# A graph network kernel: the second layer's first two pairs of tiles are taken into the first stage

## The reference

```python
def gat_conv(x, src, dst, W, a_src, a_dst, bias):      # H = 4 heads, C = 256
    h = (x @ W).reshape(n, H, C)
    al_s = jnp.einsum('nhc,hc->nh', h, a_src)
    al_d = jnp.einsum('nhc,hc->nh', h, a_dst)
    e = jax.nn.leaky_relu(al_s[src] + al_d[dst], NEG_SLOPE)
    ...                                                # softmax over the edges of each dst: alpha
    out = jax.ops.segment_sum(h[src] * alpha[:, :, None], dst, num_segments=n)
    return out.reshape(n, H * C) + bias
...
h = jax.nn.relu(gat_conv(x, src, dst, W1, a_src1, a_dst1, b1))   # src, dst with a self loop per node
h = jax.nn.relu(gat_conv(h, src, dst, W2, a_src2, a_dst2, b2))
return h @ Wfc + bfc
```

## Time and profile before

| | before |
|---|---|
| median of 3 runs | 2270.3 us (2266.53 to 2275.2) |
| the profiled execution | 2270.06 us |
| its span in the profile | 2268.0 us |
| PE busy | 2203.5 us (97%) |
| DVE busy | 1487.4 us (66%) |
| ACT busy | 1017.8 us (45%) |
| POOL busy | 944.5 us (42%) |
| mean granted clock of PE | 0.989 |

### The profile page before, as it was taken

One profiled execution on the slowest core, in us unless ns is written; L12 is line 12 of the kernel. 1 busy time (PEld: TensorE's weight loads), 2 busy tenths in 40 slices (PEclk: granted clock), 3 DMA queues, 4 the chain that ended last, 5 costly groups with the idle time before them and its releaser, 6 DMA issues.

```text
span 2268.0 us, 36374 instructions
## 1 busy us (share of the span) xinstructions
PE 2203.5 (97%) x12269; PEld 1889.0 (83%) x12269; DVE 1487.4 (66%) x4613; ACT 1017.8 (45%) x2024; POOL 944.5 (42%) x931
## 2 busy tenths in 40 slices
PE   7999999979999999999999999999999999999996
PEld 6878788858899888888999999988888777888785
DVE  7777778755667856666435665277776766677675
ACT  4982112222356632222224665334344665666454
POOL 2017637745222234366542222023545553652542
PEclk9999999989999999999999999999999999999998
DMA  6334575443476748787225666356667776776532
GB/s 211 140 136 138 133 203 193 163 138 105 137 246 216 272 158 275 258 284 244 86 88 187 214 233 237 126 195 210 229 206 255 239 241 218 242 249 222 170 123 65
DMA packets 192479, 435.82 MB, mean 192 GB/s; under 512 B 45735, under 2 KB 74606, under 8 KB 191758
## 3 DMA queue, kind: packets, MB, share of 16 engines
q1 hardware_dynamic: 127018, 249.08, 32.0%
q0 software_dynamic: 65296, 184.67, 26.2%
HBM read 242.68 MB, written 190.96 MB: 191 GB/s over the span
## 4 chain that ended last, share of the span: by engine, by line
PE 70%; DVE 4%; ACT 2%; issue 2%; DMA 1%; POOL 0%; ACTq 0%; DVEq 0%; SPq 0%; POOLq 0%
PE g_h_ps L2587 7%; PE g_h_ps L2604 7%; PE g_h_ps L2589 7%; PE g_h_ps L2588 7%; PE g_h_ps L2605 6%; PE g_h_ps L2606 6%; PE g_h_ps L2629 5%; PE g_h_ps L2631 5%; PE g_h_ps L2630 5%; PE g_t_ps L80 4%; PE g_h_ps L1759 2%; PE g_h_ps L1761 2%; PE g_h_ps L1760 2%; PE g_sum_ps L999 1%; PE g_sum_ps L998 1%
## 5 line engine op out<-in xcount | busy, mean ns | idle before, releaser
L2726 ACT ACTIVATE g_act_t<-g_t_ps,g_b_col 128x256 f32<-128x256 f32 (+1 forms) x488 | 202.2, 467 | 394.4 <-PE g_t_ps L80 394.2
L2604 PE MATMUL g_h_ps<-g_x_hi,held_w_hi 128*128 128x256 f32 x1216 | 352.1, 290 | 0.0
L2605 PE MATMUL g_h_ps<-g_x_lo,held_w_hi 128*128 128x256 f32 x1216 | 343.9, 283 | 0.0
L2606 PE MATMUL g_h_ps<-g_x_hi,held_w_lo 128*128 128x256 f32 x1216 | 343.7, 283 | 0.0
L610 DVE CUSTOM_DVE_ANT_0 g_prod<-g_h_sb,g_a_rows 128x256 f32<-128x256 f32 x632 | 224.2, 421 | 77.8 <-ACT g_h_sb L501 70.2
L2629 PE MATMUL g_h_ps<-fc_w_hi,g_x_hi 128*128 128x512 f32 x632 | 268.4, 425 | 3.2 <-DVE fc_z L3012 2.5
L2587 PE MATMUL g_h_ps<-held_w_hi,g_x_hi 128*128 128x512 f32 x656 | 263.5, 402 | 0.0
L2589 PE MATMUL g_h_ps<-held_w_hi,g_x_lo 128*128 128x512 f32 x656 | 256.8, 391 | 0.0
L2588 PE MATMUL g_h_ps<-held_w_lo,g_x_hi 128*128 128x512 f32 x656 | 256.6, 391 | 0.0
L432 PE MATMUL g_h_ps<-g_w_hi,g_x_hi 128*128 128x512 f32 x616 | 243.3, 395 | 8.6 <-DVE g_x_lo L596 6.5
L2631 PE MATMUL g_h_ps<-fc_w_hi,g_x_lo 128*128 128x512 f32 x632 | 247.3, 391 | 0.0
(11 more groups left out here) (399 smaller groups left out, 4838.3 us busy)
## 6 DMA issues: line engine op xcount, KB each, us to landing
h<-g_h_sb SPq DMA_DIRECT2D x120, 512.0 KB, 3.9
g_x_in<-in_dram SPq DMA_DIRECT2D x40, 512.0 KB, 4.0
h<-g_rows_own SPq DMA_DIRECT2D x40, 512.0 KB, 4.9
h_cols<-g_h_sb SPq DMA_DIRECT2D x38, 512.0 KB, 4.2
xb_rows<-in_dram SPq DMA_DIRECT2D x19, 1024.0 KB
xb<-xb_rows SPq DMA_DIRECT2D x19, 1024.0 KB, 4.4
g_x_in<-h_cols SPq DMA_DIRECT2D x38, 512.0 KB, 7.2
g_x_in<-h SPq DMA_DIRECT2D x21, 512.0 KB, 5.5
```

Source lines behind the costliest of these rows:

```text
L2604: pe.matmul(out, wh, xh, start=(k == 0), stop=False)
L2605: pe.matmul(out, wh, xl, start=False, stop=False)
L2606: last = pe.matmul(out, wl, xh, start=False, stop=(k == KC - 1))
```

## The change

1. Tiles 74 to 77 (two pairs without edges) now come first in `order`. Stage 1 gathers their rows of h1 itself, at its end, after `held.perm` has landed. Node numbers in these slots are bounded (under 5,888), so the gather waits only for the stores of the first 46 tiles.
2. PE transposes the first pair between T77 and T78, and after T78 computes halves 0 and 1 of stage 2 into two PSUM banks that both stages hold. Stage 2 starts with half 2. The second pair's rows stay in SBUF and are transposed in halves 2 and 3.
3. The identity, the biases and two banks are allocated for both stages; `a_rows` of stage 2 is loaded at half 4, since its place is still in use.
4. DVE does the attention of T0 and T1 before it handles the second row of edge ends.
5. In pass i = 9 DVE splits m = 20 ahead of the 16 dot products of m = 18.

```diff
+FILLS = HC // P // 2
+FIRST = 2
+FIRST_TILE = TILES - 1 - 2 * FIRST
+FIRST_ROWS = -(-(NP + ENDS * P + TILES - FIRST_TILE * P) // P) * P
...
             @block.gpsimd                                # dense_and_prep
...
                 pool.wait_ge(perm_in, 16)
+                pool.wait_ge(w2_lo_done, KC2)
+                for q in range(4):
+                    pool.wait_ge(h_stored[q], 16 * len(range(q, FIRST_ROWS // P, 4)))
+                for m, rows in enumerate((first_x, held.next_x)):
+                    for j in range(2):
+                        at = held.perm[:, FIRST_TILE + 2 * m + j, ROW1:ROW1 + 1].bitcast(I32)
+                        pool.indirect_dma_start(rows[:, j, :], None, h_out[0:FIRST_ROWS],
+                                                bass.IndirectOffsetOnAxis(at, 0)).then_inc(first_in[m], 16)
+                pool.wait_ge(first_in[1], 32)
...
             @block.tensor
...
-                body(PASSES - 1)
+                def turn_first(f):
+                    for c in range(2):
+                        for j in range(2):
+                            k = 2 * f + c
+                            last = turn_whole(pe, flat_ps[f][:, c * G + j * P:c * G + (j + 1) * P],
+                                              first_x[:, j, k * P:(k + 1) * P], held.ident_r[:, :])
+                    last.then_inc(first_turned, 1)
+                def first_columns(n):
+                    out = held.ps[n]
+                    for c in range(2):
+                        part = slice((2 * n + c) * P, (2 * n + c + 1) * P)
+                        for k in range(KC2):
+                            if n == 0 and c == 0 and k % 2 == 0:
+                                pe.wait_ge(first_lo_done, k // 2 + 1)
...
+                            pe.matmul(cols, wh, xh, start=(k == 0), stop=False)
+                            pe.matmul(cols, wh, xl, start=False, stop=False)
+                            pe.matmul(cols, wl, xh, start=False, stop=(k == KC2 - 1))
+                products(MACROS - 2, PASSES - 1, 0)
+                pe.wait_ge(first_in[0], 32)
+                for f in range(FILLS):
+                    turn_first(f)
+                products(MACROS - 1, PASSES - 1, 1)
+                pe.wait_ge(w2_lo_done, KC2)
+                for n in range(2):
+                    first_columns(n)
...
             @block.scalar
...
-                body(PASSES - 1, 0, 0)
+                for j in range(2):
+                    evac(MACROS - 2, PASSES - 1, 0, j)
+                act.wait_ge(b_in, 32)
+                for f in range(FILLS):
+                    relu_first(f)
+                evac(MACROS - 1, PASSES - 1, 1, 0)
...
             @block.vector
...
                 for o in range(2):
                     if o == 1:
                         splits(2, 1, 0)
+                        dve.wait_ge(a_in, 16)
+                        attention(0, 0, 0)
                     dve.wait_ge(rows_in[o], 16)
...
-                dve.wait_ge(a_in, 16)
...
                 tie(0, 1)
-                body(0, ahead=2)
+                attention(1, 0, 1)
...
                 use_factors(3)
-                body(RANKED + 4, ahead=1)
+                splits(2 * (RANKED + 4) + 2, RANKED + 5, 0)
+                body(RANKED + 4, ahead=2)
...
-                body(PASSES - 1, last=True)
+                splits(MACROS - 1, PASSES - 1, 1)
+                attention(MACROS - 2, PASSES - 1, 0, [0])
+                for f in range(FILLS):
+                    split_first(f)
+                attention(MACROS - 2, PASSES - 1, 0, [1])
+                attention(MACROS - 1, PASSES - 1, 1)
...
                                                          # node_layers
-    order = [*range(EARLY_A), *range(ENDS, ENDS + EARLY_B), *range(EARLY_A, ENDS), *range(ENDS + EARLY_B, TILES)]
+    early_end = ENDS + EARLY_B - 2 * FIRST
+    order = [*range(FIRST_TILE, FIRST_TILE + 2 * FIRST), *range(EARLY_A), *range(ENDS, early_end),
+             *range(EARLY_A, ENDS), *range(early_end, FIRST_TILE), *range(FIRST_TILE + 2 * FIRST, TILES)]
...
+        if m == 0:
+            return [(k, f) for i, k, f in ((2, 2, 0), (2, 6, 1), (3, 2, 2), (3, 6, 3)) if i == h]
...
+                    if h == first_half[1]:
+                        sp.wait_ge(filled, FILLS * FIRST)
+                        sp.dma_start(a_rows[:, :, :], avec.partition_broadcast(P)).then_inc(a_in, 16)
...
-                gather(0)
+                gather(FIRST)
                 constants()
-                gather(1)
...
-                pe.wait_ge(const_done, 3)
+                pe.sem_inc(tile_done, 2)
+                pe.sem_inc(filled, FILLS)
...
-                for f in range(FILLS):
-                    fill(0, f)
-                for h in range(GH):
+                for h in range(2, GH):
                     products(h)
```

More of the change, by code:

```diff
@@ L194, in dense_and_prep @@
         hid = sb("hid", [F + 1, EP])
+        hid_end = sb.end
         yr = sb("yr", [P, 7, ET])
@@ L197, in dense_and_prep @@
              for buffer in (row[0], row[1], signs[0]) for n in range(2)]
+        first = Space(nc, "first", first_at)
+        held.first_lo = first("lo", [P, KC2, G], F32R)
+        first_act = Space(nc, "first", first.end)("act", [P, 2, HC])
+        first_x = first("x", [P, 2, HC])
+        held.first_hi = first("hi", [P, KC2, G], F32R)
+        assert first.end <= hid_end
+        held.next_x = Space(nc, "first", held.end)("next_x", [P, 2, HC])
+        held.first_at, held.first_end = first_at, first.end
         h_ps = [ps(f"h_ps{s}", [P, HC]) for s in range(2)]
-        f_ps = [ps(f"f_ps{s}", [P, PER, 4 * F]) for s in range(4)]
+        flat_ps = [held.ps[0][:, :], held.ps[1][:, :], *(ps(f"f_ps{s}", [P, 512])[:, :] for s in range(2))]
+        f_ps = [bank.rearrange("p (t k) -> p t k", t=PER) for bank in flat_ps]
         w_in = [sem(f"g1_w_in{s}") for s in range(2)]
@@ L249, in dense_and_prep @@
         u_stored = sem("filt_u_stored")
+        b_in = sem("first_b_in")
+        first_in = [sem(f"first_in{m}") for m in range(FIRST)]
+        first_turned = sem("first_turned")
+        first_relu = sem("first_relu")
+        first_hi_done = sem("first_hi_done")
+        first_lo_done = sem("first_lo_done")
         CONST = 9
@@ L567, in _, with relu_first @@
                     body(i, 0, 0)
-                body(PASSES - 1, 0, 0)
+                def relu_first(f):
+                    act.wait_ge(first_turned, f + 1)
+                    for c in range(2):
+                        k = 2 * f + c
+                        last = act.activation(first_act[:, c, f * G:(f + 1) * G], flat_ps[f][:, c * G:(c + 1) * G], ACT.Relu,
+                                              bias=held.b_col[:, 0, k:k + 1])
+                    last.then_inc(first_relu, 1)
+                for j in range(2):
[4 more added lines that the diff above has]
+                evac(MACROS - 1, PASSES - 1, 1, 0)
             @block.vector
@@ L630, in body @@
                     attention(2 * i, i, 0)
-                    if not last and ahead < 2:
+                    if ahead < 2:
                         splits(2 * i + 2, i + 1, 0)
@@ L2029, in node_layers @@
         e.cut = early("cut", [H, EP + 1])[:, :]
-        assert early.end <= fwd_at
+        assert early.end <= min(fwd_at, held.first_at)
         e.fwd = Space(nc, "g2", fwd_at)("fwd", [H, EP])[:, :]
@@ L2237, in loads @@
         def loads(m, j):
-            return len([n for n in range(m + 1) if n % 2 == m % 2 and j < len(units(n)) and by_pool(n) == by_pool(m)])
+            return len([n for n in range(FIRST, m + 1) if n % 2 == m % 2 and j < len(units(n)) and by_pool(n) == by_pool(m)])
         def x1_landed(m):
@@ L2797, in finish_y @@
                     last.then_inc(y_done, 1)
-                for f in range(FILLS):
-                    relu(0, f)
                 def beside(g):
@@ L3052, in _ @@
                 dve.tensor_copy(e.key_col[:, :], tabs[:, :, KEY]).then_inc(key_set, 1)
-                for f in range(FILLS):
-                    split(0, f)
-                dve.wait_ge(a_in, 16)
-                dve.wait_ge(const_done, 3)
+                dve.sem_inc(hi_done, FILLS)
+                dve.sem_inc(lo_done, FILLS)
+                dve.wait_ge(const_done, 1)
                 dve.wait_ge(key_set, 1)
```

82 lines of the change are left out of this document (46 added, 36 removed).

## The result

| | kernel before | changed kernel |
|---|---|---|
| median | 2270.29 us (12 runs) | 2277.58 us (2270.72 to 2284.18, 12 runs) |
| profiled execution | 2270.06 us | 2272.55 us |
| its span | 2268.0 us | 2270.8 us |
| ratio to before | | 1.0029, 95% interval 1.0021 to 1.0038 |

The change makes the kernel 0.29% slower. I had forecast 2259.0 us, with a range of 2255 to 2265: wrong in the direction and outside the range. "Slower" as such had 0.02, by another mechanism.

What follows compares the result with a forecast made beforehand. PE, busy 97% of the span, was taken as the bound. PE ahead by 14.4 us at the gather, +1.7 at the passage and +1.6 at half 4 gave -11.1 us from 2270.06: 2259.0 us, range 2255 to 2265.

Steps and rivals of the forecast that it cites:

- "Slower" as such: Whole kernel: slower by over 0.5%, through edge scoring becoming the bound; chance 0.02.
- The matmuls cost nothing more: Stage 2: as many column pairs are left out later as are added at the passage, so 0 us.
- Edit 4: Head of stage 1: early dot products of T0 and T1 bring the rank chain and PE 0.7 us earlier.
- Edit 5: Pass i = 9: 5.5 us saved at T40, but marks hold T52, which waits 5.1 us at low clock: +2.5 us.
- The gather: End of stage 1: table lands at 458.8, PE transposes from 466.7 after 1.4 us idle; PE ahead by 14.4 us.
- The passage: Between the stages: last store's landing and 0.3 us to PE's first matmul add 1.7 us to PE.
- Half 4: Start of half 4 in stage 2: PE waits 1.6 us for the split behind the last transposes of m = 1.
- The clock falls once more: Rival: idle before the first transposes or at the passage passes 2 us; 2261 to 2265, say 2262.5; chance 0.21.
- The edge scores: Rival at half 12: DVE's scoring waits for POOL's 40 gathers and splits queue behind; 2271 at least when slower; chance 0.04.
- one large entry: PE's waits in the kernel before: only the passage between the stages is large; other stage 1 waits are 0.6 to 3.0 us.

Runs made afterwards that it cites:

- e5: Changed kernel with 128 bytes free behind the held tiles and 128 more ahead of the edge rows' block, r_i in the gap; 2265.12 us, ratio 0.9966.
- e2: Kernel before with 128 bytes left free behind the held tiles, nothing else; 2277.11 us, ratio 1.0031.
- e7: e5 with DVE's key-border search moved from half 3 to half 5 and the first pair's transposes inside T78; 2254.40 us, ratio 0.9917.
- e10: e7 with the second pair's four groups of transposes spread closer to the start of half 2; 2255.76 us, ratio 0.9931.
- e12: Kernel before with 64 bytes left free behind the held tiles; 2276.55 us in a single execution.
- e1: Changed kernel with 128 bytes left free behind the held tiles, nothing else; 2270.08 us, ratio 0.9994.
- e11: e10 with the split of m = 26 ahead of DVE's wait for marks; 2251.41 us, ratio 0.9914, one execution of 8967.9 us left out.

## Why the prediction was wrong, point by point

- **The edits left out of the sum.** I took the identity, the biases and the two banks, which are now allocated for both stages, as free. They were the most expensive part: some 14 us by the ratios of e5 and the changed kernel, 10.0 us between the two profiles. "The matmuls cost nothing more" is the step that failed: they start 233.4 ns apart in layer two instead of 227.9, because the distance of x tiles and weights changed. Without it the change would have been faster, as forecast, by 0.3% and not by 0.5% (e5); the direction of the forecast failed at this one term.
- **Edit 4.** Mis-sized, and read from the wrong engine: the 0.7 us were ACT's idle time ahead of T6's copy, put down to the dot products. It is PE that waits, for the split behind them, 0.8 us in before and 2.4 when T5 runs at full clock. In the two profiles the ranks came 4.0 us earlier: 2.3 for this (ACT's idle time there in e2), 0.9 because T0 was copied earlier in that execution, 0.7 because ACT's counting began earlier.
- **Edit 5.** "+2.5 us" was wrong, and so would -5.5 have been: it is 0 within 0.13%. I treated the 10.2 us that POOL waited for its scatters, and with it the end of the marks' wait at 310.09, as fixed. In the changed kernel POOL waited 6.6 us, and the marks' wait ended at 301.81, 8.3 us earlier. The mechanism exists: T52 waited 1.9 us in e5, 1.8 in e7 and 2.7 in e10, at the low clock, and in these three T42 waited too. It is not in every run, and the wait is about half of the 5.1 us of the forecast, or less.

```profile
301.81 0.20 DVE L873 TENSOR_SCALAR g_kind<-g_marks 128x79 f32<-128x79 f32 x1 [5.30 <-DMA g_marks<-map_s]
```

- **The gather.** The chain was right: table read at 441.15, first gather 11.5 us later (I had 11.1), PE's start 7.4 us after that (7.1 + 0.8). The table's read and the end of T77 moved together and are 14.0 us apart as before, so PE waits from 14.0 to 11.5 + 7.4 = 18.9 us behind the read: 5.0 us. The low clock comes on top: the 16 transposes take 2.0 us, where the sum has 1.2, and T78's first three matmuls are 0.42 to 0.56 us apart. My delay of T52 and the earlier landing, which did not come, had left 1.4. By the fit of the Trainium skill (DMA: Bandwidth & Descriptors, Anatomy of one DMA) the table takes an estimated 2.4 us, and there would have been no wait; the 11.5 us between these two rows do not agree with it.
- **The passage**: 1.7 us were forecast, 481.56 - 479.92 = 1.6 measured.
- **Half 4**: 1.6 us forecast, 4.7 and the low clock measured. I asked for the way from transposes to split and not for what DVE has queued ahead of the split: the key borders, behind a wait for a DMA. With them moved the wait is 1.34.
- **The rivals.** "The clock falls once more" happened, twice, and was not what decided. The edge scores never bound anything: no wait of PE between half 4 and the end of layer two.
- **The account in the profiles.** 17.7 us ahead at 481.56; 4.7 go at half 4, some 2.6 in the 5.2 us at the low clock behind it, 10.0 by the places. By this estimate 0.4 would be left, and the changed kernel is 2.8 behind: some 3 us are not accounted for. Nor does "one large entry" among PE's waits hold for before: it also waits 9.4 us at the start for its weights, as the changed kernel does (9.5), which changes nothing in the sum.

## What to carry to other kernels

An allocation is an edit. Where a change shifts tiles in SBUF, compare the pace of the matmuls in untouched stages before and after, and where 512 columns stream, try a distance of a matmul's two SBUF operands that is a multiple of 256 bytes; here it was 0.6% of the kernel. A wait in one profile is the wait beside that execution's other losses: look at the same place in a second execution before it is priced. And where an engine is to do something sooner, list what stands ahead of it in that engine's queue, waits for DMAs first.

## What the runs showed of the hardware

- 512-column fp32 matmuls with their weight load start 226.8 ns apart in stage 1, where x tile and weights lie a multiple of 256 bytes apart; in layer two it is 227.9 at such a distance and 233.4 when they are 64 or 128 off (before, e12, e2): 2.4%. With 256 columns it is the reverse, 119.7, 118.8 (128) and 116.5 (64). The Trainium skill (TensorE: Matmul & The Clock Gate, Step-by-step: what each phase is for) says that PE has two independent SBUF read ports and that loading the next weights takes nothing from the running matmul's reads. In e1, e2, e5 and e12 the pace depends on where the two operands lie relative to each other, which that sentence would not lead one to expect. That the two reads disturb each other is a guess, and why 256 bytes, no run here tells.
- After the transposes of a group the pace is slower for about six matmuls in the kernel before (timeline around 902 us) and then returns to 226.7; in the changed kernel, in most halves, starts 229 and 237 ns apart go on in turn to the end of the half.
- The length of a short idle time did not decide whether the clock fell. PE was idle 2.06 us ahead of T5 in before and in e2: low clock in the first, full clock in the second, where the copy starts 5.87 us behind PE's start. It was idle 1.96 us ahead of T26 in e1 and in e10: low clock in the first (7.38 us), full in the second (5.75). And T52 in e5 ran at the low clock after 1.92 us, T54 in e11 at full clock after 2.44. ACT's copy, which ends the tile, shows it, 7.4 us after PE's start in e5

```profile
317.49 0.49 PE L469 MATMUL g_h_ps<-g_w_hi,g_x_hi 128*128 128x512 f32 x1 [1.92 <-DVE g_x_lo L678]
```

```profile
324.87 1.03 ACT L569 ACTIVATE g_h_sb<-g_h_ps 128x1024 f32<-128x1024 f32 x1 [8.61 <-PE g_h_ps L471]
```

and 5.75 in e11:

```profile
325.95 0.49 PE L471 MATMUL g_h_ps<-g_w_hi,g_x_hi 128*128 128x512 f32 x1 [2.44 <-DVE g_x_lo L681]
```

```profile
331.70 1.03 ACT L572 ACTIVATE g_h_sb<-g_h_ps 128x1024 f32<-128x1024 f32 x1 [7.13 <-PE g_h_ps L473]
```
